# A four-layer transformer on one core: the setup of attention's start, with weight rounding and slot constants at another place

## The reference

```python
def _weight_fake_quant(w):
    scale = jnp.max(jnp.abs(w), axis=1, keepdims=True) / QMAX
    return jnp.clip(_ste_round(w / scale), -QMAX - 1.0, QMAX) * scale
# layer 1, feed-forward: w_gate and w_up are 352 x 128, w_down is 128 x 352
xq = _act_fake_quant(x, clip_x[0])
gate = jnp.einsum('bsh,ih->bsi', xq, _weight_fake_quant(w_gate))
up = jnp.einsum('bsh,ih->bsi', xq, _weight_fake_quant(w_up))
h = _act_fake_quant(jax.nn.silu(gate) * up, clip_down[0])
out = jnp.einsum('bsi,hi->bsh', h, _weight_fake_quant(w_down))
# layer 2, slots: the parts that hang on no token
S = slot_init * slot_scale; slot_mean = S.mean(axis=0)
gh = hs @ gru_whh.T + gru_bhh
route_logits = (h @ w2.T + b2) / (jnp.abs(tau) + 0.1)
```

## Time and profile before

| | |
|---|---|
| three runs | 2115.42, 2119.77, 2124.47 us (median 2119.77) |
| profiled execution | 2117.64 us, its span 2115.9 us |
| mean granted TensorE clock | 0.957 |
| TensorE busy | 1859.6 us, 88% of the span |
| VectorE busy | 1486.2 us, 70% |
| ScalarE busy | 1302.6 us, 62% |
| POOL busy | 616.5 us, 29% |
| first instruction of block 2's attention | 34.25 us |
| first instruction of block 3 | 835.97 us |

### The profile page before, as it was taken

How to read it: one execution, slowest core, us unless ns; L and a number is a source line. 1 busy time by engine, 2 the same in 40 slices (tenths; PEclk the granted TensorE clock), 3 DMA queues, 4 the chain that set the end, 5 groups by cost and what they waited for, 6 DMA issues and landing times.

```text
span 2115.9 us, 49981 instructions
## 1 busy us (share of the span) xinstructions
PE 1859.6 (88%) x17665; PEld 1511.9 (71%) x17669; DVE 1486.2 (70%) x3873; ACT 1302.6 (62%) x4466; POOL 616.5 (29%) x610
## 2 busy tenths in 40 slices
PE   3998999989999897577898889999999998898879
PEld 2777888878888775455666677787777777677665
DVE  5898887878888785757666675767757565654556
ACT  1987766656667786456577766667666654544432
POOL 0003031322322220034333343254452523233321
PEclk9999999999999999868699999999999999999999
DMA  8013455444644001300000011222222223232351
GB/s 245 17 31 105 126 163 156 134 136 140 181 133 127 26 26 50 110 20 20 30 7 15 7 46 50 83 75 89 79 74 69 76 87 91 71 103 70 110 155 43
DMA packets 128789, 178.44 MB, mean 84 GB/s; under 512 B 10144, under 2 KB 89824, under 8 KB 128288
## 3 DMA queue, kind: packets, MB, share of 16 engines
q1 hardware_dynamic: 120864, 159.51, 25.0%
q0 software_dynamic: 7680, 15.74, 2.4%
HBM read 141.26 MB, written 33.95 MB: 83 GB/s over the span
## 4 chain that ended last, share of the span: by engine, by line
PE 38%; DVE 9%; ACT 6%; issue 4%; POOL 1%; DMA 0%; DVEq 0%; ACTq 0%; SPq 0%
PE ps L1674 5%; PE ps L1959 5%; PE ps L1907 3%; PE ps L1712 3%; PE ps L1900 3%; ACT pb L2108 3%; PE ps L1696 3%; PE ps L1881 2%; PE ps L1703 2%; PE ps L1685 2%; PE ps L1722 1%; DVE nm L2487 1%; PE ps L1730 1%; PE ps L1929 1%; PE ps L1873 1%
## 5 line engine op out<-in xcount | busy, mean ns | idle before, releaser
L2108 ACT ACTIVATE pb<-ps,nm 128x128 f32<-128x128 f32 x1024 | 363.1, 377 | 192.6 <-DVE nm L2487 192.5
L2156 POOL TENSOR_TENSOR pb<-pb,rcs 128x512 f32<-128x512 f32 x256 | 268.3, 1049 | 667.1 <-DVE rcs L2495 666.2
L986 ACT ACTIVATE pb<-pb,nm 128x128 f32<-128x128 f32 x1024 | 312.9, 393 | 30.9 <-DVE nm L1221 29.1
L2512 DVE COPY pt<-ps 128x512 f32<-128x512 f32 x128 | 88.3, 690 | 203.6 <-PE ps L1959 203.4
L2108 ACT ACTIVATION_READ_ACCUMULATOR pb<-ps,nm 128x1 f32 x1024 | 221.3, 216 | 0.0
L2487 DVE TENSOR_REDUCE nm<-ps 128x8 f32<-128x1024 f32 x128 | 155.9, 1218 | 62.2 <-PE ps L1907 39.0
L1959 PE MATMUL ps<-w,pb 128*128 128x128 f32 x1024 | 168.7, 290 | 21.9 <-ACT pt L2116 10.8
L1221 DVE TENSOR_REDUCE nm<-pb 128x8 f32<-128x1024 f32 x128 | 156.2, 1220 | 4.4
L1959 PEld LDWEIGHTS ps<-w,pb 128*128 128x128 f32 x1024 | 122.4, 148 | 46.3 <-ACT pt L2116 20.3
L870 PE MATMUL ps<-w,pb 128*128 128x128 f32 x1024 | 141.8, 280 | 8.2 <-ACT pb L986 7.9
L2116 ACT ACTIVATE pt<-ps 128x512 f32<-128x512 f32 x128 | 76.9, 601 | 94.9 <-PE ps L1959 94.6
(11 more groups left out here) (379 smaller groups left out, 4405.0 us busy)
## 6 DMA issues: line engine op xcount, KB each, us to landing
big<-in_we SPq DMA_DIRECT2D x92, 514.0 KB
big<-in_we SPq DMA_DIRECT2D x109, 384.0 KB
sorted_out<-big SPq DMA_DIRECT2D x27, 256.0 KB
big<-sorted_in SPq DMA_DIRECT2D x7, 960.0 KB, 5.7
sorted_in<-big SPq DMA_DIRECT2D x4, 1472.0 KB, 12.1
big<-sorted_in SPq DMA_DIRECT2D x20, 256.0 KB, 3.8
hidden<-h_all SPq DMA_DIRECT2D x7, 512.0 KB, 3.0
h_all<-hidden SPq DMA_DIRECT2D x7, 512.0 KB, 3.7
```

The source lines that it names most:

```text
L986: m = a.activation(pb[:, n % 2, k * S:(k + 1) * S], pb[:, n % 2, k * S:(k + 1) * S], ACT.Exp, bias=nm[:, n % 2, k:k + 1])
L2108: m = a.activation(pb[:, n % 2, e * S:(e + 1) * S], ps[:, score_bank(n) + half, k * S:(k + 1) * S], ACT.Exp, bias=nm[:, n % 2, e:e + 1], a ...
L2156: g_.tensor_tensor(p4, p4, r4.unsqueeze(2).to_broadcast([P, 4, S]), ALU.mult).then_inc(n2["p_normed"], 1)
L2512: v.tensor_copy(pt[:, p % 2, 4 * S:8 * S], ps[:, BANK_T, :]).then_inc(n2["p_lo"], 1)
```

## The change

SP's first block issues only two loads: x of group 0 (256 KB) and the first 136 columns of `w` (the identity and the two head masks, moved to the front). Block 1 keeps of VectorE's work only three small fills, of TensorE's and ScalarE's nothing. All other loads are issued by SP in block 2, behind the loads of group 0 and ahead of those of group 1; the zeros for `sorted_in` follow at n = 0 of SP. `xs0` is filled by POOL at the head of block 2, ahead of its first power. TensorE turns the identity twice before its first real turn. The statistics of group 1 move from turn 0 to turn 1, its power and its apply from turn 1 to turn 2, and VectorE waits there for `large_loaded`. Rounding stands in turns 3, 4, 5, 6, 7, 9 and 10 at place 3, the turn of each piece on TensorE at place 0 of the next turn, the copy at place 2 of the next turn; the diagonal in turns 11 and 12. The slot constants stand in turns 128, 129 and 130, the sigmoids in turn 131. The pieces use slots 0 to 3 of `hT` and PSUM bank 5 (banks 0 and 1 for the slots).

```diff
-W_COLS = [("ident", 128), ("wo0", 128), ("wr0", E0), ("b2_0", 128),
+W_COLS = [("ident", 128), ("hm", 4), ("hms", 4), ("wo0", 128), ("wr0", E0), ("b2_0", 128),
...
+W_FIRST = 128 + 4 + 4
...
             def _(sp):
-                sp.dma_start(w[:, :], w_d).then_inc(small_loaded, 16)
-                sp.dma_start(rows[:, :], r_d.partition_broadcast(P)).then_inc(small_loaded, 16)
-                for k, src in enumerate((wg_d, wu_d)):
...
-                sp.dma_start(x_all[:, :, :], x_d.rearrange("b s d -> s b d")).then_inc(large_loaded, 16)
-                sp.dma_start(big[:, CONST:CONST + RANK_CONST], rank_d).then_inc(large_loaded, 16)
-                sp.wait_ge(sorted_zero, 1)
...
-                sp.wait_ge(large_loaded, 16 * n_large)
+                sp.dma_start(x_all[:, 0:G, :], x_d.rearrange("b s d -> s b d")[:, 0:G, :]).then_inc(first_loaded, 16)
+                sp.dma_start(w[:, 0:W_FIRST], w_d[:, 0:W_FIRST]).then_inc(first_loaded, 16)
...
+        WEIGHTS_AT = [3, 4, 5, 6, 7, 9, 10]
+        DIAG_AT = WEIGHTS_AT[-1] + 1
+        SLOTS_FROM = NUN
...
                 loads(0)
+                sp.dma_start(x_all[:, G:B, :], x_d.rearrange("b s d -> s b d")[:, G:B, :]).then_inc(large_loaded, 16)
+                sp.dma_start(w[:, W_FIRST:W_N], w_d[:, W_FIRST:W_N]).then_inc(small_loaded, 16)
+                sp.dma_start(rows[:, :], r_d.partition_broadcast(P)).then_inc(small_loaded, 16)
+                for k, src in enumerate((wg_d, wu_d)):
+                    for c, (at, m) in enumerate(CH1):
+                        sp.dma_start(weight(3 * k + c), src[at:at + m, :]).then_inc(small_loaded, 16)
+                sp.dma_start(weight(6), wd_d).then_inc(small_loaded, 16)
+                sp.dma_start(big[:, CONST:CONST + RANK_CONST], rank_d).then_inc(large_loaded, 16)
                 for n in range(NUN):
...
+                    if n == 0:
+                        sp.wait_ge(sorted_zero, 1)
+                        for g in range(NP):
+                            sp.dma_start(xs_d[g].rearrange("(t p) d -> p t d", p=P), xs0[:, :, :]).then_inc(xs_zeroed, 16)
...
+                    if n == WEIGHTS_AT[0] and place == 0:
+                        pe.wait_ge(small_loaded, 16 * n_small)
+                        pe.wait_ge(large_loaded, 16 * n_large)
+                    if n - 1 in WEIGHTS_AT and place == 0:
+                        t = WEIGHTS_AT.index(n - 1)
+                        m, src = weight_rows(t), rounded_weight(t)
+                        pe.wait_ge(w_rounded, 1 + t + 1)
...
+                        i.then_inc(w_turned, 1)
...
+                    if n == SLOTS_FROM + 1 and place == 2:
+                        pe.wait_ge(slots_ready, 1)
+                        pe.transpose(ps[:, 0, 0:P], hs_c[:, :], ident)
+                        pe.matmul(ps[:, 0, P:P + 1], hs_c[0:SLOTS, :], ones[0:SLOTS, 0:1], start=True, stop=True)\
+                            .then_inc(slots_psum, 1)
+                    if n == SLOTS_FROM + 2 and place == 2:
+                        pe.wait_ge(slots_ready, 2)
+                        pe.matmul(ps[0:HR, 1, 0:1], W("w1m"), smean[:, :], start=True, stop=True)
+                        pe.matmul(ps[:, 1, P:P + 3 * D], hsT[:, :], W("whh"), start=True, stop=True).then_inc(slots_psum, 1)
+
+                pe.wait_ge(first_loaded, 32)
+                for i in range(2):
+                    pe.transpose(ps[:, 4, i * P:(i + 1) * P], ident, ident)
                 turn_y(front, 1, (front.yT_ready, 1))
...
+                    if n == NUN + 3 and place == 2:
+                        a.activation(sc[:, 6:7], R("clip_x"), ACT.Sigmoid)
+                        a.activation(sc[:, 7:8], R("clip_down"), ACT.Sigmoid)
...
+                g_.memset(xs0[:, :, :], 0.0).then_inc(sorted_zero, 1)
                 pow_(front, 1)
...
-                    if layer == 0 and u == 1:
+                    if n == WEIGHTS_AT[0]:
+                        g_.wait_ge(small_loaded, 16 * n_small)
+                    if layer == 0 and u == (1 if j else 2):
                         pow_(front, g + 1)
...
-                    if n == 0 and place == 3:
+                    if n == 1 and place == 3:
+                        v.wait_ge(large_loaded, 16 * n_large)
                         stats(front, 1, 2)
...
-                    if layer == 0 and here == (3, 1):
+                    if layer == 0 and here == (3, 1 if j else 2):
                         v.wait_ge(front.yT_psum, g)
                         apply(front, g, g + 1)
...
+                    if place == 2 and n - 1 in WEIGHTS_AT:
+                        keep_weight(WEIGHTS_AT.index(n - 1))
+                    if place == 3 and n in WEIGHTS_AT:
+                        if n == WEIGHTS_AT[0]:
+                            v.wait_ge(small_loaded, 16 * n_small)
+                        round_weight(WEIGHTS_AT.index(n))
+                    if place == 3 and n == DIAG_AT:
+                        v.tensor_scalar(diag, ident, sc[:, 0:1], None, ALU.mult).then_inc(diag_ready, 1)
+                    if place == 2 and n == DIAG_AT + 1:
+                        v.wait_ge(scales_psum, 1)
+                        v.tensor_copy(dscB[:, :], ps[:, 5, 0:P])
+                    if place == 3 and n - SLOTS_FROM in range(3):
+                        slot_constants(n - SLOTS_FROM)
...
+                v.wait_ge(first_loaded, 32)
                 stats(front, 0, 1)
                 apply(front, 0, 1)
                 queries(0, (front.yT_ready, 1), W("hm"))
+                v.tensor_copy(identb[:, :], ident).then_inc(w_rounded, 1)
```

More of the change, by code:

```diff
@@ L836, in work @@
                         tile(*item)
+                    if n == WEIGHTS_AT[0] and place == 0:
[5 more added lines that the diff above has]
+                        pe.wait_ge(w_rounded, 1 + t + 1)
+                        if t < 6:
+                            i = pe.transpose(weights_turned[:, 0:m], src[:, 0:D], identb[0:m, 0:m])
+                        else:
+                            for c, (at, mc) in enumerate(CH1):
+                                i = pe.transpose(weights_turned[0:mc, c * P:(c + 1) * P], src[:, at:at + mc], identb[:, :])
+                        i.then_inc(w_turned, 1)
+                    if n == DIAG_AT + 1 and place == 0:
+                        pe.wait_ge(diag_ready, 1)
+                        pe.matmul(ps[:, 5, 0:P], ones[:, :], diag, start=True, stop=True).then_inc(scales_psum, 1)
+                    if n == SLOTS_FROM + 1 and place == 2:
[10 more added lines that the diff above has]
+                    pe.transpose(ps[:, 4, i * P:(i + 1) * P], ident, ident)
                 turn_y(front, 1, (front.yT_ready, 1))
@@ L961, in work @@
                         tile(*item)
+                    if n == WEIGHTS_AT[0] and place == 0:
+                        a.wait_ge(small_loaded, 16 * n_small)
+                    if n == NUN + 3 and place == 2:
+                        a.activation(sc[:, 6:7], R("clip_x"), ACT.Sigmoid)
+                        a.activation(sc[:, 7:8], R("clip_down"), ACT.Sigmoid)
                 a.wait_ge(front.yT_psum, 1)
@@ new lines, in keep_weight, with slot_constants @@
+                def keep_weight(t):
+                    m = weight_rows(t)
+                    v.wait_ge(w_turned, t + 1)
+                    if t < 6:
+                        at = CH1[t % 3][0]
+                        v.tensor_copy((wgq if t < 3 else wuq)[:, at:at + m], weights_turned[:, 0:m])
+                    else:
+                        for c, (at, mc) in enumerate(CH1):
+                            v.tensor_copy(wdq[0:mc, c, :], weights_turned[0:mc, c * P:(c + 1) * P])
+                def slot_constants(step):
+                    if step == 0:
+                        wlink(v.tensor_scalar(sc[:, 4:5], R("tau"), -1.0, None, ALU.mult))
+                        wlink(v.tensor_tensor(sc[:, 4:5], sc[:, 4:5], R("tau"), ALU.max))
+                        wlink(v.tensor_scalar(sc[:, 4:5], sc[:, 4:5], 0.1, None, ALU.add))
+                        v.reciprocal(sc[:, 5:6], sc[:, 4:5])
+                        v.tensor_scalar(hs_c[:, :], W("slot"), W("slot_scale"), None, ALU.mult).then_inc(slots_ready, 1)
+                    if step == 1:
+                        v.wait_ge(slots_psum, 1)
+                        v.tensor_copy(hsT[:, :], ps[:, 0, 0:P])
+                        v.tensor_scalar(smean[:, :], ps[:, 0, P:P + 1], 1.0 / SLOTS, None, ALU.mult).then_inc(slots_ready, 1)
+                    if step == 2:
+                        v.wait_ge(slots_psum, 2)
+                        v.tensor_tensor(c1[0:HR, :], ps[0:HR, 1, 0:1], W("b1s", HR), ALU.add)
+                        wlink(v.tensor_tensor(crz[:, :], ps[:, 1, P:P + 2 * D], R("bhh")[:, 0:2 * D], ALU.add))
+                        v.tensor_tensor(crz[:, :], crz[:, :], R("bih")[:, 0:2 * D], ALU.add)
+                        wlink(v.tensor_tensor(hn_c[:, :], ps[:, 1, P + 2 * D:P + 3 * D], R("bhh")[:, 2 * D:3 * D], ALU.add))
```

(1 more changed line is left out.)

96 lines of the change are left out of this document (21 added, 75 removed).

## The result

The changed kernel took 2099.88 us (median of 20 runs, 2088.75 to 2109.25), the kernel before on the same chip 2112.89 (20 runs, 2106.4 to 2124.47). The ratio is 0.9936, with an interval of 0.992 to 0.9952: 13 us faster. The profiled execution of after took 2107.22 us (span 2105.4, mean granted clock 0.955), 10.4 less than that of before.

A forecast was written before the change was run, and what follows sets the result against it. ScalarE was taken to bound the units (3.8 us of its own work each), with a serial start and drain. Terms -29.65 + 1.0 + 9.0 + 3.7 = -16.0 on the profiled 2117.64 gave 2101.6, forecast 2102 us, range 2095 to 2113.

The forecast's parts named there:

- start: Before attention: first statistics wait only for two small loads, at 4.6 instead of 34.25 us: -29.65 us.
- wait for the data: Unit 1: VectorE waits for rank, last on the queue, landing near 22 us: +1.0 us, between 0 and 5.
- rival A: Units 4, 7 and 9: late VectorE idles TensorE, whose clock falls three times by 3 us: +9, 2110.6 us; chance 0.22.
- rounding itself: Units 3 to 10: 14 us of added VectorE work, partly absorbed by its free time: +9.0 us, bounds 6 to 14.
- slot constants, with their clock fall: Drain after unit 127: constants lengthen the serial chain by +3.7 us, sigmoids hidden, products at full clock; no fall foreseen.
- C: Added work hides in VectorE's free time: rounding 6, drain 2, data nothing; -21.6 us or more, 2096 to 2093; chance 0.15.
- The prediction's own sign for A: Units 3 to 12: granted clock 0.50 in two or three stretches, instead of 1.00, would mean the clock falls.
- The rule on turns as activity for the clock: TensorE in the rounding units: turns do not count as products do, so fillers and scores must hold the clock; no size.
- B: From the start through rounding, TensorE stays at 1.2 GHz, 7.1 us a unit: +17, 2135 us; chance 0.04.
- D: Start not freed: first statistics at 10 us, or remaining data at 28: +5 to +6, 2107 us; chance 0.09.

The follow-up runs named there:

- e1: Changed kernel, but VectorE's wait in unit 1 is for the rest of x alone, no longer for rank: 2104.86 us, one execution.
- e2: Changed kernel with the slot constants in units 18 to 20 instead of the drain: 2096.66 us, one execution.
- a1: The changed kernel itself, unaltered, timed again beside three variants on one chip: 2099.55 us, ratio 0.9937 to the kernel before.
- e6: Changed kernel with both the wait for x alone and the slot constants in units 18 to 20: 2091.21 us, ratio 0.9858 to the kernel before.
- e7: e6 with three rounding instructions on POOL and each weight turn, its copy and the diagonal one unit later: 2084.11 us, ratio 0.983 to the kernel before.
- a4: Same kernel as e7, timed on the chip of a1: 2087.48 us, ratio 0.9875 to the kernel before.
- a2: Same kernel as e1 (wait for x alone), timed on the chip of a1: 2091.16 us, ratio 0.9904 to the kernel before.
- e8: e7 with nine extra identity products on TensorE in the head: 2085.92 us, ratio 0.9832 to the kernel before.
- a3: Same kernel as e2 (slot constants in units 18 to 20), timed on the chip of a1: 2095.56 us, ratio 0.9918 to the kernel before.
- e3: Changed kernel with rounding's multiply-add, subtract and clip moved from VectorE to POOL, turns not delayed: 2104.98 us, one execution.
- e4: Changed kernel with extra TensorE products: nine in the head, four ahead of the weight turns in units 5, 8 and 10: 2109.93 us, one execution.
- e5: Changed kernel with most rounding instructions left out (clip, turns and copies stay; integer weights not the reference's): 2089.22 us, one execution.

## Why the prediction came out right

The forecast was 2102 us, the sum -16.0 on the profiled execution, a ratio of 0.9924; measured were 2099.88 and 0.9936. So the sum is 2.5 us too favourable against the ratio (which makes 13.5 of 2117.64), and the absolute time agrees better than it should, since the kernel before itself ran 6.9 us below the earlier median. The sum hit in part by luck, because errors of both signs balance:

| term | predicted | measured | by |
|---|---|---|---|
| start | -29.65 | -30.8 | mark of unit 0 |
| unit 2 at the low clock | 0 | +1.9 | e1 at unit 4, against before |
| wait for the data | +1.0 | +2.0 | e1 against after at unit 3 |
| clock fall behind it | 0 (rival A) | +2.9 | e1 against after at unit 4 |
| rounding itself | +9.0 | +5.7 | units 4 to 13, falls taken out |
| clock fall in it | 0 (rival A) | +1.5 | the rest of 7.2 |
| slot constants, with their clock fall | +3.7 | +4.05 | e2 |
| sum | -16.0 | -12.7 | ratio: -13.5 |

The last column takes single pairs of traces; a1 shows how far they carry: by unit 4 it is 2.0 us ahead of after, and in units 4 to 13 1.3 us behind it. The -12.7 leaves out the +3.0 and -5.3 of the two common stretches.

*Start.* Right, at 3.79 in place of 4.6. The x load landed 2.6 us after its issue, not the 3.8 of the earlier trace rows, which is the median of later loads of that size. Here the fit of the Trainium skill (DMA: Bandwidth & Descriptors, Anatomy of one DMA), 2.6 us for 256 KB, was the better figure, and the trace agrees with it, though the page gives the fit for the software queue and these loads went over the hardware one; for the 68 KB load it gives 2.2, measured 2.5.

*Low clock in unit 2.* By duration TensorE worked at the low level from 11.1 to some 25 us in after, through the scores of units 0, 1 and 2; before, unit 2's were quick. It varies among the six kernels that wait for x alone. Where unit 2's scores took 1.16 (e6, e7), unit 4's mask add stands at 29.10 and 29.45, and nothing is lost against before (60.10 - 30.8 = 29.3); at 1.44 (a4) it stands at 29.59, at 2.08 (e1, a2, e8) at 30.87 to 31.16. So the low clock is the 1.9. Why it lasts in some profiles is open.

*Data wait.* The mechanism was right (rank, last on the queue, releases VectorE at unit 1) and the place too; the load landed at 24.0, the prediction said 22, and so the wait was 4.90 in place of 1 to 2 us. The step that failed is the price of the wait, "+1.0, between 0 and 5". It counted only VectorE's lateness, and missed that a late VectorE leaves TensorE idle and that the clock falls behind it: 2.9 us in this pair of traces on top of the wait's own 2.0 (1.6 and 1.4 in a1 and a2). Rival A had the mechanism, but looked for it at the rounding.

*Rounding.* The sum put 14 us on VectorE's 29.5 of nine units. Over units 3 to 11 its busy time rose by 10.1 (29.54 to 39.66). The added instructions' own durations sum to some 12; in these full units their rows overlap, and the 14 had also counted the gaps between the instructions of a serial setup. Taking for each unit the shortest time in any of the eight kernels with this rounding gives 47.9 us for units 4 to 13, 5.7 over before: just under the lower bound that I had given, and C's figure of 6. Unit 3 itself hid its piece (4.20 against 4.14 in e1). Units 4, 5, 7, 9 and 10 pay 0.8 to 1.5 each; for 4, 7 and 9, where queries, statistics or apply stand beside a piece, this was foreseen. Unit 4 was forecast at 6 us: 5.91. The nine units 3 to 11, forecast at 45, took 46.1, but 3.0 of that is unit 3's fall and not rounding.

*Rival A* came in part: two falls in after, 2.9 and 1.5 us, where it had three of 3 us, and the larger stands behind the wait. The windows of 2 us from 28 to 90 us sort all thirteen changed kernels. The seven that wait for rank (after, a1, a3, e2, e3, e4, e5) all fall in 28 to 34 us; the six that wait for x alone (e1, a2, e6, e7, e8, a4) do not. Behind 36 us after, a1, a2, a3, e1, e3 and e6 fall; the three with late POOL rounding (e7, e8, a4) and e5 do not, and e2 and e4 did not either, so there it varies from profile to profile. Two more falls of after lie outside these windows: at unit 20 (0.50 from 114 to 116 us, the unit takes 7.87 us, before 6.21) and in the drain. The prediction's own sign for A, 0.50 in two or three stretches, was met. The rule on turns as activity for the clock that the prediction cited is not tested: e4 and e8 add products, and none takes the turns away.

*Drain.* The number is right, 4.05 for 3.7, and the sigmoids are hidden as said. But the 3.7 put TensorE's products there at full clock, and they ran at the low one: with some 1.4 of the 4.05 for the fall (e6), the constants alone would be nearer 2.6, an estimate. *B* was far off. *C* was right on the rounding and wrong on the rest. *D* did not occur.

## What to carry to other kernels

Let a wait ask for the one transfer that its reader needs, not for the last of the queue: here that is worth 1.4 to 2.0 us of waiting and 1.6 to 2.9 of clock. When VectorE becomes late on the path of a TensorE that runs by fillers, price the clock too, and give the work to an idle engine only with a turn of slack, since the same three instructions on POOL made ten units 3.3 us slower without it and 5.3 faster with it, both against after. Don't make the front faster while a load is behind it (e4). Whether products placed in the wait itself would hold the clock was not run.

## What the runs showed that I had not expected

- The granted clock column and the durations part ways at the start: windows of 10 to 24 us say 1.00 in after, and the scores in them take 2.07 and 2.08 us, as at the low level (20.00:22.00 above, with scores at 19.89). A first stretch has to be read by durations.
- An issue of a 1547 KB load held SP 6.83 us, and everything queued behind it, rank included, came that much later.
- The clock fell to 0.50 behind two gaps of 1.14 and 1.12 us (after) as it did in one of 5.13 (e4), and stayed up from 24 to 52 us in e1, which had neither.
- POOL's steps on 128x128 took 0.37, 0.53 and 0.29 us, against 0.29, 0.23 and 0.23 on VectorE: slower, but on an engine that had 1.9 us of other work in these ten units.
- The same pair of kernels gave a ratio of 0.983 (0.98 to 0.986) on one chip and 0.9875 (0.9849 to 0.99) on another. The intervals just overlap, so a difference between chips is not shown, but parts of 4 us are better compared side by side on one chip.
